# A selective-scan block with FFN: output and FFN blocks built up in PSUM on their residual rows, dt, B and C summed over a chunk in the same bank

## The reference

```python
h = layernorm(x)
xs, z = split(h @ in_proj_w)                  # 2048 channels each
xc = silu(causal_conv4(xs) + conv_b)
ssm = xc @ x_proj_w.T                         # 64 + 16 + 16 columns: dt, B, C
dt_r, B, C = rmsnorm of each of the three
dt = softplus(dt_r @ dt_proj_w.T + dt_bias)
state[t] = exp(dt * A) * state[t-1] + dt * B * xc      # 16 states per channel
y = (sum over states of C * state + D * xc) * silu(z)
x = x + y @ out_proj_w.T                      # output projection
x = x + layernorm(x) @ dequantised_w.T + bias # FFN
```

## Time and profile before

| | |
|---|---|
| median of three executions | 4658.65 us (4651.46 to 4660.2) |
| the profiled execution | 4652.27 us, its span 4650.4 us |
| busy: PE, DVE, POOL, ACT | 95%, 90%, 87%, 76% |
| one chunk of the steady loop (c = 3 to 14) | 275.5 us: last step 36.89, first 38.4 to 39.9, six others 33.20 each |

### The profile page before, as it was taken

The page is one execution under the profiler, slowest core; times in us unless marked ns, Lnnn a source line. Parts: engine busy times, 40 slices in busy tenths (PEclk is TensorE's granted clock), DMA queues, the critical chain, the costliest instruction groups (busy, mean ns, idle before and its releaser), DMA issues.

```text
span 4650.4 us, 80289 instructions
## 1 busy us (share of the span) xinstructions
PE 4425.4 (95%) x26656; PEld 4020.1 (86%) x26656; DVE 4164.3 (90%) x5745; ACT 3537.7 (76%) x8848; POOL 4034.5 (87%) x2942
## 2 busy tenths in 40 slices
PE   7788999999999999999999999999999999998879
PEld 6577889989898998989899898998989899897769
DVE  3899999999999999999999899999999999999871
ACT  3787787877878787787878878787887878777650
POOL 0898989989899998989899899999989999899870
PEclk9889999999999999999999999999999999999889
DMA  7324344353544435353444535335353443533232
GB/s 252 135 82 160 104 156 147 121 184 129 184 137 159 147 129 179 137 181 128 150 156 137 186 122 184 128 131 191 120 184 129 175 144 115 184 129 135 96 106 84
DMA packets 160286, 678.57 MB, mean 146 GB/s; under 512 B 21120, under 2 KB 30080, under 8 KB 110720
## 3 DMA queue, kind: packets, MB, share of 16 engines
q1 hardware_dynamic: 141440, 639.88, 39.6%
q10 hardware_dynamic: 18432, 33.56, 1.9%
HBM read 618.32 MB, written 55.05 MB: 145 GB/s over the span
## 4 chain that ended last, share of the span: by engine, by line
PE 65%; DVE 14%; POOL 8%; issue 7%; DMA 3%; ACT 2%; SPq 1%; POOLq 0%; DVEq 0%; ACTq 0%
PE gx L594 15%; PE ys L574 13%; PE g L767 12%; PE ys L614 12%; DVE hb L1378 9%; PE g L689 6%; POOL dbx L486 5%; DVE hc L1326 3%; POOL half L494 2%; PE ys L604 2%; PE ys L624 2%; PE hb L875 1%; DVE gx L1270 1%; DMA b_scratch<-ssmT 1%; DMA ybuf<-in_wf_scales 1%
## 5 line engine op out<-in xcount | busy, mean ns | idle before, releaser
L1378 DVE TENSOR_TENSOR_SCAN hb<-hb,dbx 128x512 f32<-128x512 f32 x2048 | 2496.7, 1219 | 110.8 <-ACT hb L1083 77.2
L486 POOL TENSOR_TENSOR dbx<-dtx,bb 128x1024 f32<-128x1024 f32 x1024 | 2421.2, 2364 | 68.9 <-DVE hb L1378 43.9
L1083 ACT ACTIVATE hb<-dt,a_neg 128x256 f32<-128x256 f32 x4096 | 1789.3, 468 | 66.3
L494 POOL TENSOR_TENSOR half<-hc 128x512 f32<-128x512 f32 x1024 | 1305.3, 1275 | 86.0 <-DVE hc L1326 85.1
L1326 DVE TENSOR_TENSOR hc<-hb,cb 128x512 f32<-128x512 f32 x2048 | 1376.2, 672 | 0.0
L574 PE MATMUL ys<-half,ident 128*128 128x256 f32 x4096 | 1057.2, 390 | 115.4 <-POOL half L494 99.1
L574 PEld LDWEIGHTS ys<-half,ident 128*128 128x128 f32 x4096 | 764.1, 194 | 242.9 <-POOL half L494 131.4
L767 PEld LDWEIGHTS g<-wo,ybuf 128*128 128x128 f32 x7680 | 909.3, 194 | 27.5 <-issue 15.2
L614 PE MATMUL ys<-xnT,wz 128*128 128x256 f32 x4096 | 931.5, 381 | 1.3 <-DVE ybuf L1337 1.3
L594 PE MATMUL gx<-xnT,wx 128*128 128x256 f32 x3968 | 903.6, 382 | 21.8 <-issue 11.0
L767 PE MATMUL g<-wo,ybuf 128*128 128x128 f32 x7680 | 915.0, 277 | 9.0 <-issue 9.0
(11 more groups left out here) (105 smaller groups left out, 2739.1 us busy)
## 6 DMA issues: line engine op xcount, KB each, us to landing
wz<-in_win SPq DMA_DIRECT2D x128, 1024.0 KB, 4.8
wx<-in_win SPq DMA_DIRECT2D x124, 1024.0 KB, 4.8
wo<-in_wout SPq DMA_DIRECT2D x123, 1024.0 KB, 5.0
wf<-wf_scratch SPq DMA_DIRECT2D x113, 512.0 KB, 3.9
xc_scratch<-xcn ACTq DMA_DIRECT2D x128, 256.0 KB, 3.7
xcs<-xc_scratch SPq DMA_DIRECT2D x128, 256.0 KB, 5.0
bb<-bc_scratch SPq DMA_DIRECT2D x64, 512.0 KB, 8.8
cb<-bc_scratch SPq DMA_DIRECT2D x64, 512.0 KB, 8.0
```

Source lines behind the costliest of these rows:

```text
L486: nc.gpsimd.tensor_tensor(dbx[:, k % 2, :].rearrange("p (n t) -> p n t", n=NQ), dtx[:, S % 2, a, :].unsqueeze(1).to_broadcast([P, NQ, T]), ...
L494: nc.gpsimd.tensor_tensor(half[:, k % 4, :], hc[:, k % 2, 0:HALF], hc[:, k % 2, HALF:GW], ALU.add).then_inc(halves, 1)
L1083: ins = nc.scalar.activation(h[:, m * T:(m + 1) * T], dt[:, j % 2, a, :], ACT.Exp, scale=a_neg[:, ds((2 * j + a) * N + 2 * v + m, 1)])
L1378: nc.vector.tensor_tensor_scan(h[:], h[:], dbx[:, k % 2, w * UW:(w + 1) * UW], 0.0, ALU.mult, ALU.add).then_inc(scans, 1)
```

## The change

PSUM takes over the three additions of DVE. An output or FFN block starts from its residual rows: ACT copies them into `g1` (`block_in`), PE accumulates onto them (no `start` flag), and ACT copies the sum back into the rows (`block_out`). The x projections of a chunk accumulate in other columns of the same bank; ACT zeroes these once per chunk (`zero_sums`) and takes them out once (`chunk_square`). Four identity matmuls at the start mark all columns of `g1` as written. All users of `g1` follow each other by semaphores: FFN matmuls, x projection, then on ACT `blocks_between` (FFN block out, in the last step the sums, output block in), output matmuls, and `out_out` and `ffn_in` at ACT's end of the step.

PE's order within a step changes too: the x projection comes right behind `late_group(7)`, and in an ordinary step three of the four parts of the output block move behind group 3.

```diff
 ACT, new functions
+            ssm_sums = g1[:, T:T + TT * E].rearrange("p (t e) -> p t e", t=TT)
+            def zero_sums():
+                nc.scalar.activation(g1[:, T:T + TT * E], ident[:, 0:1].to_broadcast([P, TT * E]), ACT.Identity,
+                                     scale=0.0).then_inc(ssm_zero, 1)
             def chunk_square(chunk):
-                act.wait_ge(xp_add, after(PAIRS * (chunk + 1)))
-                nc.scalar.activation(sq[:], ssm[:], ACT.Square).then_inc(rms_sq, 1)
+                act.wait_ge(xp_mm, after(PAIRS * (chunk + 1)))
+                nc.scalar.activation(sq[:], ssm_sums, ACT.Square).then_inc(rms_sq, 1)
+                act.wait_ge(rms_ready, after(chunk))
+                nc.scalar.copy(ssm[:], ssm_sums).then_inc(ssm_out, 1)
+                act.wait_ge(rms_sq, after(chunk + 1))
+                act.wait_ge(ssm_out, after(chunk + 1))
+                zero_sums()
+            def block_in(chunk, col, done):
+                nc.scalar.copy(g1[:, 0:TT * P].rearrange("p (t h) -> p t h", t=TT), block_rows(chunk, col)
+                               ).then_inc(done, 1)
+            def block_out(chunk, col, done):
+                nc.scalar.copy(block_rows(chunk, col), g1[:, 0:TT * P].rearrange("p (t h) -> p t h", t=TT)
+                               ).then_inc(done, 1)
+            def ffn_out(S):
+                k = S - 2 * PAIRS
+                act.wait_ge(f_mm, after(k))
+                block_out((k - 1) // PAIRS, (k - 1) % PAIRS, f_out)
...
+                    def blocks_between():
+                        if st.inproj:
+                            act.wait_ge(xp_mm, after(S + PAIRS + 1))
+                        if st.before(first).ffn:
+                            ffn_out(S)
                         if last and st.inproj:
                             chunk_square(c + 1)
+                        if st.outproj:
+                            act.wait_ge(xres_in, landed(c))
+                            act.wait_ge(f_out, after(S - 2 * PAIRS))
+                            block_in(c - 1, j, o_pre)
+                    def out_out():
+                        if st.outproj:
+                            act.wait_ge(o_mm, after(S - PAIRS + 1))
+                            block_out(c - 1, j, o_out)
+                    def ffn_in():
+                        if st.ffn:
+                            act.wait_ge(o_out, after(S - PAIRS + 1))
+                            act.wait_ge(bias_add, after((S - 2 * PAIRS) // 2 + 1))
+                            block_in(c - 2, j, f_pre)
 ACT, order of a step
                     unit(5)
                     norm1(1)
+                    blocks_between()
                     unit(6)
...
                     norm1(3)
-                    rms_square()
+                    rms_apply()
                     unit(8)
                     norm2(0)
-                    rms_apply()
...
                     second_skip_term()
+                    if last:
+                        out_out()
                     unit(14)
...
                     unit(15)
+                    if not last:
+                        out_out()
+                    ffn_in()
 SP, first step
-                        sp.wait_ge(f_add, after(PAIRS * (c - 2)))
+                        sp.wait_ge(f_out, after(PAIRS * (c - 2)))
                         sp.dma_start(out_rows[c - 3], x2_rows(1 - st.parity)).then_inc(out_st, 16)
 PE
             def pair_proj(q):
...
-                        mm = nc.tensor.matmul(ys[1][:, tt * E:(tt + 1) * E],
+                        mm = nc.tensor.matmul(g1[:, T + tt * E:T + (tt + 1) * E],
...
-                            g1_after_o()
+                        pe.wait_ge(f_pre, after(S - 2 * PAIRS))
...
                     def x_proj():
                         if st.inproj:
-                            if was.scan and not (first and c == 0):
-                                pe.wait_ge(y_ready, after(2 * S))
...
+                            pe.wait_ge(o_pre, after(S - PAIRS + 1))
...
                     ffn()
                     late_group(6)
                     late_group(7)
+                    x_proj()
                     if last and st.norm1:
                         norm1(0)
-                        x_proj()
-                        out_proj(0)
                         norm1(1)
                         group(0)
+                        out_proj(0)
                         norm1(2)
                         out_proj(1)
                         norm1(3)
...
                         group(2)
+                        dt_proj()
                         group(3)
-                        dt_proj()
                         out_proj(2)
                         out_proj(3)
                     elif first and st.ffn:
                         out_proj(0)
+                        group(0)
                         out_proj(1)
-                        x_proj()
-                        group(0)
                         out_proj(2)
                         norm2(0)
                         out_proj(3)
...
                     else:
+                        x_in_proj(0)
+                        group(0)
                         out_proj(0)
-                        out_proj(1)
-                        x_proj()
-                        group(0)
-                        x_in_proj(0)
                         group(1)
                         ss_transpose()
                         x_in_proj(1)
                         group(2)
                         group(3)
                         dt_proj()
+                        out_proj(1)
                         out_proj(2)
                         out_proj(3)
                     z_in_proj(1)
 DVE: pair_ss, add_x_proj, add_ffn and add_out are gone
-                    add_ffn()
...
-                    add_x_proj()
...
-                    add_out()
-                    norm_stats()
                     scan(14)
                     product(13)
+                    norm_stats()
```

More of the change, by code:

```diff
@@ L412, in store_columns @@
                 h = slice(half * H // 2, (half + 1) * H // 2)
-                sp.wait_ge(f_add, after(PAIRS * chunk + (half + 1) * PAIRS // 2))
+                sp.wait_ge(f_add, after(PAIRS * (chunk - NC + 2) + (half + 1) * PAIRS // 2))
                 sp.dma_start(out_rows[chunk][:, :, h], x2_rows(chunk % 2)[:, :, h]).then_inc(out_st, 16)
@@ L423, in _ @@
             load_wf(0)
-            sp.wait_ge(f_add, after(LAST - 2 * PAIRS))
+            sp.wait_ge(f_out, after(LAST - 2 * PAIRS))
             sp.dma_start(out_rows[NC - 3], x2_rows((NC - 3) % 2)).then_inc(out_st, 16)
@@ L634, in _ @@
             pe.wait_ge(id_ready, after(1))
+            for m in range(4):
+                mm = nc.tensor.matmul(g1[:, m * P:(m + 1) * P], ident[:], ident[:], start=(m == 0), stop=True,
+                                      skip_group_check=True)
+            mm.then_inc(g1_marked, 1)
             pe.wait_ge(l1_ready, after(2))
@@ L645, in _ @@
             for q in range(2, PAIRS):
-                if q > 2:
-                    pe.wait_ge(xp_add, after(q - 2))
                 pair_proj(q - 2)
@@ L650, in _ @@
                     pair_in_proj(q, a)
-            pe.wait_ge(xp_add, after(PAIRS - 2))
             pair_proj(PAIRS - 2)
@@ L654, in _ @@
             pair_z(0, 1)
-            pe.wait_ge(xp_add, after(PAIRS - 1))
             pair_proj(PAIRS - 1)
@@ L709, in x_proj @@
                         if st.inproj:
-                            if was.scan and not (first and c == 0):
-                                pe.wait_ge(y_ready, after(2 * S))
-                            else:
-                                pe.wait_ge(xp_add, after(S + PAIRS))
+                            if was.outproj and not was.ffn:
+                                pe.wait_ge(o_out, after(S - PAIRS))
                             pair_proj(S + PAIRS)
@@ L769, in out_proj @@
                                                            (kt % 2) * T + tt * P:(kt % 2) * T + (tt + 1) * P],
-                                                      wo[:, kt, :], start=(kt == 0 and tt == 0),
+                                                      wo[:, kt, :], start=False,
                                                       stop=(kt == TILES - 1), skip_group_check=True)
@@ L785, in ss_transpose @@
                         if last and st.inproj:
+                            pe.wait_ge(y_ready, after(2 * S))
                             chunk_ss(c + 1)
@@ L854, in ffn_block @@
                 pe.wait_ge(l2_evac, after(4 * (chunk + 1)))
-                pe.wait_ge(f_add, after(k - 1 if j else k))
+                n = k - (NC - 2) * PAIRS
+                pe.wait_ge(f_add, after(n - 1 if j else n))
+                if n == 0:
+                    pe.wait_ge(f_out, after(LAST - 2 * PAIRS))
                 bank = (g1, gx)[j % 2]
@@ L882, in _ @@
             pe.wait_ge(wf_in, landed(LAST - 2 * PAIRS))
-            pe.wait_ge(o_add, after(LAST - PAIRS))
```

(28 more changed lines are left out.)

52 lines of the change are left out of this document (16 added, 36 removed).

## The result

The changed kernel takes 4947.81 us (median of 4 runs, 4945.53 to 4953.22), the kernel before 4656.39 in the same session: ratio 1.0628, 95% interval 1.061 to 1.0647. The forecast was 4950. The profiled execution after has a span of 4946.0 us, before 4650.4.

What follows compares the result with a forecast made beforehand. PE's work was taken to bound the 78 ordinary steps, so only new waits on PE's order matter. Terms 58 + 178 + 11 + 11 + 27 + 10 - 4 + 2 = +293 gave 4950 us, range 4850 to 5030.

Steps and rivals of the forecast that it cites:

- Ordinary steps: 78 steps of chunks 2 to 14: PE reaches group 3 before half(3) is ready, waits 0.75 us each, +58 us.
- The rival that ordinary steps stay at 33.20: Round trip as forecast, but no new wait in ordinary steps: 4892 us, chance 0.15.
- First steps: ACT waits for a store and a load of 1 MB, delaying the output block: +14.8 us a step, times 12 = +178.
- The rival of an 11.5 us store: First steps: the store still takes its median 11.5 us, 6 us more in 13 chunks: 5028 us, chance 0.12.
- One of its bounds: First steps: the store lands no earlier than 15.3 us, since no 1 MB transfer here takes under 5.0.
- The clock: First steps: PE idle for 14 us falls to the lower clock level, +2.7 us a step, bounds 0 and 4.
- Last steps: PE waits for ACT's evacuations and the block: 38.9 instead of 36.89 us, +2.0 in 13 chunks, +27 in all.
- ACT's copies: Four copies of 256 elements on ACT, 0.38 us each, 1.5 us in 7.2 spare, lying beside other work.
- Chunk 14's last step: Counted with the other last steps: +2.0 us from PE's waits for ACT.
- Chunk 15's first step: Same chain of store and load as other first steps, with less PE work: +11 us.
- The start and the end: Chunks 1 and 2 +4 and +7 us, chunks 0 and 1 -4, last FFN block behind the loop +2.
- The busy times: Over the whole run: DVE's busy time down by some 130 us, ACT's up by some 170.

Runs made afterwards that it cites:

- Experiment 1: Changed kernel with output part 1 back ahead of group 3 in ordinary steps: 4866.87 us, ratio 1.0454.
- experiment 2: Kernel before with output part 1 moved behind dt in ordinary steps, nothing through ACT: 4761.1 us, ratio 1.0228.
- experiment 3: Changed kernel with the first column block of a chunk's x rows loaded a chunk earlier into its own buffer: 4802.33 us, ratio 1.0319.
- experiment 4: Kernel of experiment 3 plus unread matmuls in first steps where PE was idle: 28 of them 4804.04 us, 14 in a second run 4768.78 us.
- experiment 5: Changed kernel with the FFN block copied out behind ACT's unit 3 in first steps, so the store is issued earlier: 4941.6 us, ratio 1.062.
- experiment 8: Changed kernel with first and ordinary steps repaired, plus last steps reordered on ACT and PE: 4680.41 us, ratio 1.0061.
- experiment 9: Kernel of experiment 8 with SP's load of the next x weights behind the loads of B and C in last steps: 4659.19 us, ratio 1.0014.
- the second run of experiment 4: Kernel of experiment 3 plus 14 unread matmuls instead of 28 in first steps: 4768.78 us, ratio 1.0254.

## Why the prediction was right

- **Ordinary steps, forecast +0.75, measured +0.88.** Each position was met: `late_y` at 5.50, `half(3)` done at 18.18 (18.19 forecast), PE at 17.47 (17.49), group 3 at 18.23 (18.24). Experiments 1 and 2 show the cause. The term was sized 0.13 short. The restart after a wait is not free: the group behind the wait is 0.97 us from the next start instead of 0.87, and x in-projection takes 3.49 instead of 3.45. In 78 steps that is the 10.6 us by which the term missed; a size was off, not the mechanism. The rival that ordinary steps stay at 33.20 fell.
- **First steps, forecast +14.8, measured +14.3 on average.** The chain ACT copy, store, load, ACT copy is in the trace with each link near its forecast: 10.1 (10.3), 15.5 (15.9), 20.5, and the output block at 21.03 (21.35). Experiments 3 and 4 show what it was worth: without the wait and its clock the steps are 40.6, 1.5 over the kernel before, as the output block still starts at 10.64. The rival of an 11.5 us store fell, and experiment 5 shows why. The long time was that of the transfers ahead of the store, as the prediction took it to be. One of its bounds was badly founded: loads of 1 MB with a median of 4.8 us are in the profile before (`wz`, `wx`), and the store of chunk 15 landed in 4.0 after the change.
- **The clock, forecast +2.7, measured 2.5 to 2.85.** In the first step of chunk 7 it is 16.80 us from the output block to the x in-projection; in experiment 4, at full clock, it is 14.31, near the 14.2 of the forecast. Experiment 4 shows the term apart, 2.85 a step. What was not foreseen is that 3.44 us of idle PE cost it in full, and that 2.41 cost 2.0 in the output burst alone (experiment 8).
- **Last steps, forecast +2.0, measured +1.9.** The three waits were put at 0.85, 1.85 and 0.85, and are 0.73, 1.48 and 0.72 in the last step of chunk 6, 0.6 less together. PE's busy time was put at 35.4 and is 35.84, so two misses nearly cancel. In this kernel PE waits for the block in, which ACT does behind its instructions on the sums in the other half of the bank, so five ACT instructions stand between x projection and the output block. The Trainium skill (PSUM — Partial Sum Buffer, PSUM bank collisions raise a hardware error) says that two engines may not access one bank on the same partitions at once, even at different columns. The kernel's waits keep to it, and no run here shows what would happen otherwise. By that, sums in the same bank cost a wait; this is argued and was not tried.
- **ACT's copies, forecast 0.38 us and hidden.** They take 0.36 and 0.38 us. Experiment 1 shows them hidden in ordinary steps. The 0.40 that the prediction worked out from the Trainium skill (ScalarE: Activation LUTs, What ACT_TABLE_LOAD costs) is 0.02 to 0.04 above.
- **The small terms were less good than the sum.** Chunk 14's last step (+4.3 for +2) was put with the other last steps, but PE runs the ordinary order in it, with output part 1 behind group 3. There it waits 3.46 us for the normed sums, as before (3.63), with a low clock behind it both times, and then 2.58 for `half`, where it was 0.23:

```profile
4492.69 2.07 PE L578 MATMUL ys<-half,ident 128*128 128x256 f32 x4 [2.58 <-POOL half L498]
...
4496.27 7.18 PE L762 MATMUL g<-wo,ybuf 128*128 128x128 f32 x48
```

Experiment 1 takes 4.9 us out of this step, so the moved part is the cause. Chunk 15's first step (+15.7 for +11) was too low as well. Its store lands in 4.0 us and ACT waits 9.11 us for the rows, less than elsewhere, so the chain is not what was missed. Some 3 us of it come late in the step: behind a wait for ACT's skip term that the kernel before has too, PE's next two bursts run at the lower clock, and before they do not. Before, then after:

```profile
4267.45 1.13 PE L574 MATMUL ys<-half,ident 128*128 128x256 f32 x4 [2.87 <-ACT ys L1102]
4268.42 3.62 PE L614 MATMUL ys<-xnT,wz 128*128 128x256 f32 x16
```
```profile
4551.66 2.07 PE L578 MATMUL ys<-half,ident 128*128 128x256 f32 x4 [2.82 <-ACT ys L1130]
4553.53 5.71 PE L621 MATMUL ys<-xnT,wz 128*128 128x256 f32 x16
```

The start and the end were put too high by 4 and 5 us, the first of which is no more than the scatter of that stretch.
- **The busy times.** ACT's rose by 163 us (170 forecast). DVE's fell by 103 us where 130 were named; 0.9 us a step, the prediction's own figure, gives about 110 in some 120 steps.
- The misses are +10.6 us in ordinary steps, -6 in the twelve first steps, -1 in last steps, +9 in chunk 15 and the step ahead of it, and -4 and -5 at the two ends. They add up to 3 us. That the total came so close is luck: the terms were off by up to 11 us, some up and some down.

## What to carry to other kernels

When a result is moved to an engine whose order also feeds others, look at everything that the new instruction waits for: one copy of 0.38 us behind a store and a load of 1 MB held back exponentials, scans and matmuls for 10 us, and reading the same rows from a small buffer filled a chunk earlier removed it. Before an engine's order is changed, compute for each wait when it is reached and when it is released; a loop with 0.6 us of room loses it with one block of 1.8 us moved behind the wait. An engine made faster in one step pays only if what starts the next step comes earlier too. Read the granted clock beside the waits: in experiments 8 and 9 PE was idle for as long, and the steps differed by 20 us. And the cheapest repair may be in a third queue: the fastest kernel here, 8.6 us (0.2%) under the kernel before, came from one load moved behind two small stores and the loads of B and C on SP.

## What the runs showed of the hardware

- Idle PE of 3.44 us, with a full clock before it, was followed by 5 us at a granted clock of 0.50 and cost 2.85 us beyond the wait; 14 matmuls of no use, which filled 3.1 us of it, kept the clock at 1.00 and made the kernel 34 us faster.
- Shorter waits cost the clock too, and their length alone does not decide it. In chunk 15's first step PE waits 2.8 us for ACT's skip term in four kernels; the granted clock behind the wait is 0.50 in the kernel after (2.82) and in experiment 3 (2.82), and 1.00 in the kernel before (2.87) and in the second run of experiment 4 (2.83). Experiment 3 and that run have the same instructions in this step. What decides it was not found.
- A store of 1 MB took 5.6 us or 11 us (medians) by what the DMA engines had to do until it landed, not by its size. A store of 32 KB took 4.5 us behind 1 MB and 1.5 without. The Trainium skill (DMA: Bandwidth & Descriptors, § Queues, rings and completion order) says that each DMA engine takes the descriptors of a ring in order; the trace agrees, as the 32 KB are issued 0.4 us behind the 1 MB on the same queue.
- A PE that has to wait loses more than the profile shows as its idle time: 0.59 us in brackets, 0.76 between the starts of the groups, 0.88 in the step. The first difference is about the 0.16 by which a burst otherwise starts before the modelled end of the one before; the second, 0.12, comes behind the wait.
